# Moving the combine of expert rows ahead of the rotary products on VectorE, in the second half of an attention and mixture-of-experts kernel

## The reference

```python
xn = _layernorm(x, axis=-1)
x = x + attn(xn, W_qkv, W_o) + ffn(xn, router_w, router_b, w1, w2)
```

## Time and profile before

| | |
|---|---|
| median of 3 runs | 1364.79 us |
| profiled execution | 1371.59 us, its span 1369.8 us |
| TensorE matmul busy | 1246.6 us, 91% of the span |
| VectorE busy | 1135.5 us, 83% |
| ScalarE busy | 1118.9 us, 82% |
| GpSimd busy | 957.0 us, 70% |
| mean granted TensorE clock | 0.97 of full speed |

### The profile page before, as it was taken

The page is one execution under the profiler, slowest core; times in us unless marked ns, Lnnn a source line. Parts: engine busy times, 40 slices in busy tenths (PEclk is TensorE's granted clock), DMA queues, the critical chain, the costliest instruction groups (busy, mean ns, idle before and its releaser), DMA issues.

```text
span 1369.8 us, 46659 instructions
## 1 busy us (share of the span) xinstructions
PE 1246.6 (91%) x15156; PEld 945.7 (69%) x15157; DVE 1135.5 (83%) x3911; ACT 1118.9 (82%) x3608; POOL 957.0 (70%) x1349
## 2 busy tenths in 40 slices
PE   1537999999999999998999999899999999999998
PEld 1514677777777777667898998566766777777766
DVE  5889888888888888876777777899999998898885
ACT  6517889898898899886787887888888888888885
POOL 3116888998998889883222221788888888888885
PEclk9558999999999999998999999999999999999999
DMA  9992433333433433353444443333334333443331
GB/s 290 290 274 70 111 81 79 81 80 80 97 95 82 98 92 79 80 140 105 126 128 130 124 130 89 84 83 88 87 94 103 97 87 95 103 104 88 88 89 31
DMA packets 154041, 149.07 MB, mean 109 GB/s; under 512 B 12785, under 2 KB 113521, under 8 KB 153585
## 3 DMA queue, kind: packets, MB, share of 16 engines
q1 hardware_dynamic: 145264, 129.21, 37.4%
q0 software_dynamic: 8576, 17.33, 4.4%
HBM read 38.28 MB, written 41.09 MB: 58 GB/s over the span
## 4 chain that ended last, share of the span: by engine, by line
PE 49%; DVE 25%; issue 11%; ACT 7%; POOL 4%; DMA 3%; SPq 2%; DVEq 0%; ACTq 0%; POOLq 0%
PE bank L1171 9%; PE bank L1172 9%; PE bank L1173 8%; DVE arena L1025 7%; PE bank L1253 6%; PE bank L1242 6%; PE bank L1280 5%; ACT probs L712 4%; DVE arena L981 4%; PE bank L1264 2%; DVE inv_parts L1039 2%; DVE arena L986 2%; DVE arena L980 2%; PE bank L1281 2%; ACT arena L656 2%
## 5 line engine op out<-in xcount | busy, mean ns | idle before, releaser
L712 ACT ACTIVATE probs<-arena,neg_max 128x128 f32<-128x128 f32 (+1 forms) x1024 | 454.0, 448 | 75.9 <-DVE neg_max L1025 72.5
L1025 DVE CUSTOM_DVE_ANT_0 arena<-bank,causal 128x128 f32<-128x128 f32 (+1 forms) x1024 | 302.8, 351 | 40.5 <-PE bank L1242 37.7
L1253 PE MATMUL bank<-ident,probs 128*128 128x128 f32 x1536 | 211.4, 274 | 7.3 <-DVE probsT L1047 3.3
L1253 PEld LDWEIGHTS bank<-ident,probs 128*128 128x128 f32 x1536 | 175.8, 141 | 37.2 <-issue 12.9
L513 POOL TENSOR_TENSOR arena<-o_whole,arena 128x256 f16<-128x256 f32 x256 | 181.5, 709 | 21.1
L712 ACT ACTIVATION_READ_ACCUMULATOR probs<-arena,neg_max 128x1 f32 x1024 | 196.0, 191 | 0.0
L1172 PE MATMUL bank<-arena 128*128 (+1 forms) x864 | 184.8, 239 | 0.0
L1171 PE MATMUL bank<-arena 128*128 (+1 forms) x864 | 183.6, 239 | 0.9 <-DVE arena L1145 0.8
L1242 PE MATMUL bank<-arena 64*128 64x128 f16 (+1 forms) x3072 | 172.1, 245 | 9.7 <-DVE neg_max L1025 5.2
L1173 PE MATMUL bank<-arena 128*128 (+1 forms) x864 | 180.8, 238 | 0.0
L695 ACT ACTIVATE probsT<-bank 128x384 f32<-128x384 f32 x384 | 170.5, 480 | 0.9
(11 more groups left out here) (154 smaller groups left out, 3310.8 us busy)
## 6 DMA issues: line engine op xcount, KB each, us to landing
arena<-arena SPq DMA_DIRECT2D x256, 256.0 KB, 3.8
arena<-sorted_x_dram SPq DMA_DIRECT2D x144, 128.0 KB, 2.2
sorted_x_dram<-stage SPq DMA_DIRECT2D x6, 2304.0 KB, 17.8
sorted_y_dram<-stage SPq DMA_DIRECT2D x72, 128.0 KB, 1.8
sorted_x_dram<-stage SPq DMA_DIRECT2D x2, 2368.0 KB, 19.1
arena<-experts_dram SPq DMA_DIRECT2D x8, 512.0 KB, 6.6
out_dram<-acc SPq DMA_DIRECT2D x32, 128.0 KB
sorted_x_dram<-stage,slots POOLq DMA_INDIRECT x128
```

The lines of the kernel that those rows point to most:

```text
L712: last = nc.scalar.activation(probs[:, s % 4, at:at + w], masked[:, s % 4, at:at + w], ACT.Exp, bias=neg_max[:, s % 4, t:t + 1], scale=-1. ...
L1025: last = nc.vector.tensor_tensor_reduce(out=masked[:, (s + i) % 4, at:at + w], in0=SC[i][:, at:at + w], in1=causal[:, 2 * P - w:2 * P], sc ...
L1253: last = nc.tensor.transpose(TP[s % 2][:, k * P:(k + 1) * P], probs[:, s % 4, k * P:(k + 1) * P], ident[:])
```

## The change

On VectorE, in the second half, the combine of a period is issued directly behind `masks` and `invert` and ahead of `turn` and `o_scale`; before, it stood behind `turn`, `o_scale` and `rope_low`. The lag stays 2 (`BACK_LAG`), and the combines of `rest_of` stay where they are. In one line the constant's name takes the place of the number 2.

```diff
-                    then = past(b, p, 2)
+                    then = past(b, p, BACK_LAG)
                     if then and p % 2 == 0:
                         invert(4 * then[0] + then[1] // 2, then[1] // 2)
+                    if then and b >= MID:
+                        combine(*then)
                     for kind, j, of, u, psum in units_at(b, p):
                         if kind == "rope":
                             turn(j, u, psum, of)
...
                     for kind, j, of, u, psum in due(b, p, 2):
                         if kind == "rope" and j >= 2 and b <= MID:
                             rope_low(j, of)
-                    then = past(b, p, BACK_LAG)
-                    if then and b >= MID:
-                        combine(*then)
                     for kind, j, of, u, psum in units_at(b, p):
                         if kind == "y":
                             y_add(of, j, u, psum, at in (FORMER, TURN))
```

## The result

| | before | changed |
|---|---|---|
| median of 5 runs | 1364.79 us (1364.40 to 1366.27) | 1371.49 us (1370.76 to 1373.22) |
| profiled execution, its span | 1371.59, 1369.8 us | 1373.22, 1371.4 us |
| mean granted clock | 0.97 | 0.97 |

The ratio is 1.0048, 95% interval [1.0033, 1.0062]: slower by 6.7 us. Two later comparisons of the same two kernels gave 1.0017 [1.0005, 1.0029] and 1.0020 [1.0008, 1.0032], that is 2.3 and 2.7 us. The kernel before never again had a median as low as 1364.79: in later jobs it was 1368.34, 1367.88, 1368.27 and 1374.41. So 2 to 3 us is what repeats. I predicted +2.0 us.

The account below looks back on a forecast made before the run. TensorE bounds the second half, VectorE sets most of its losses. Per sample +0.4 us wait in p3, -0.2 transposes; 12 samples +2.4, first two -0.5: total +2, 1366.8 us, range 1353.5 to 1370.5.

Parts of the forecast that it names:

- the case in which the combine of p1 slips in: Second half, p1: combine starts 0.04 us ahead of GpSimd's L513, gets in, holds it some 0.15; likeliest case.
- The hold: VectorE's combine is held until GpSimd's instruction ends, finishing 0.14 or 0.15 us after it, rather than slowed.
- rival D: Contention is a slowdown: combine costs 0.70 us ahead of `turn` too; 1377 us; chance 0.08 together with a gather wait.
- What it saves: VectorE 0.44 us per `turn` period; L970 down to 0.34 to 0.45; TensorE's 0.2 before p3's transposes, L986 wait gone.
- What p6 and p0 pay: Combine ahead of `turn` makes `turn` 0.26 us late in p6 and 0.47 late in p0.
- rival A: In p1 the combine is held by L513; `turn` of p2 is 0.55 us late; 1368.5 us; chance 0.24.
- A's sum: Second half: 12 samples each 0.35 us longer, less 0.5 for its first two samples: +3.7, 1368.5 us.
- The bound on the masks: In p6, masks wait for TensorE; if they came 0.3 us sooner, the sum would be 3.6 lower.
- The gather: VectorE's wait for gathered rows moves up by 1.5 us at most; gather issued two periods before; costed at nothing.
- B: String breaks at p2: L1039 gets in before L513; 30.9 us a sample, 1353.5; chance 0.28 with halves of it.
- The base: Profiled execution of 1371.59 us is 6.8 above the median of 1364.79; the difference is carried over to the median.
- My own sign: Prediction is wrong if p3's output units are not 31.7 to 32.3 us apart, or TensorE stops elsewhere than p3.

Follow-up runs that it names:

- the sixteen columns: Kernel before, with a combine that adds only the first 16 of the 128 columns; one run, 1364.28 us, 31.12 us a sample.
- the run later by one: Kernel before, combines still behind `o_scale`, those of p2, p3 and p4 one period later, two in p5; 1361.53 us, ratio 0.9958.
- the second profile: Changed kernel run and profiled again with nothing edited, against the kernel before in the same job; 1370.07 us, ratio 1.0017.

## Why the prediction was right or wrong

It said 1366.8 us, +2.0 over 1364.79, by the case in which the combine of p1 slips in. Measured was 1371.49, outside the range. Point by point:

- **The hold** was right, and the sixteen columns show it by themselves. The Trainium skill has it the same way on another page than the one that rival D reads as a slowdown: it (SBUF — State Buffer, section SBUF: two separate sides) calls the shared pair an exclusive lock, held for the whole instruction, in which the loser is fully blocked. The ends 0.14 us after GpSimd's instruction agree with that.
- **What it saves**: L970 from 674 to 456 ns (I said 0.34 to 0.45 us), and the transposes' 0.2 gone (0.25 in the run later by one). Right, but part of L970's time went to L1041. The wait for L986 is another matter: where the masks are early it is 1.5 us in the kernel before and 1.6 changed, so there was nothing to save; only where they are late does it fall, from 3.9 to 1.6.
- **What p6 and p0 pay**: I had 0.26 and 0.47. Measured are 0.27 and 0.40 where the masks are early, 0.28 and 0.50 where they are late, if one takes off the 0.20 by which the masks themselves are later. Right.
- **p1 is the step that failed.** I took it that a combine starting 0.04 us ahead of L513 slips in and holds it by 0.15. The arrival was right (I had 0.03 ahead of L513, the rows show 0.02 to 0.04), the outcome not: the combine was held by L513, and L513 wasn't moved at all (0.48 after L511, 0.47 in the earlier trace rows). That is rival A, which had 0.24 of my chances, in its place, its price (`turn` of p2 0.55 late, measured 0.50) and its sign. My point from which A decides, 0.04 us later than my times, was drawn too late: a lead of 0.04 isn't enough, one of 0.06 is, and the 0.15 is then right. In the sum the step is small: `turn` of p2 is 0.50 late and not 0.4, some 1.2 us in 12 samples.
- **A's sum** was 12 x 0.35 - 0.5 = +3.7. Measured is 0.24 a sample in one kind of chip and 0.50 in the other. The 0.24 is 0.49 - 0.25, against my 0.55 - 0.2. The 0.50 has a term that I didn't have: the masks of p6 come 0.20 later than before. My reading, which no run tests, is that TensorE had lost that much in the waits for L986 and ahead of the transposes, and that with these gone its results come later behind its rows instead.
- **The bound on the masks** ("if they came 0.3 sooner, the sum would be 3.6 lower") has a right size, 0.26 x 12 = 3.1, but the wrong cause. The change doesn't move them forward; on other chips they come 0.4 us sooner in the kernel before, and 0.6 in the changed one.
- **The gather** I costed at nothing on the strength of one wait of 0.6 us. In the second profile VectorE waits for it six times, 3.2 us in 380; 1.0 to 1.4 us is passed on where the masks are early. A mis-sized term: the combine now asks up to 1.5 us sooner, and the gather of two periods before has not always landed.
- **B** was wrong in its place (L1039 of p2 starts 0.27 behind L513, not 0.10) but its pace was there to be had: 30.67 a sample, once the combines leave p0, p1 and p2 altogether and L1039 gets in ahead of L518.
- **D** falls with the sixteen columns.
- **The base.** Where the masks are late, the profile gave 31.8 us a sample and 1371.6; the median of 1364.79 belongs to other executions, which have no profile. I carried the difference over as if it were constant. Of the first 6.7 us some 3 repeat. The rest stays unexplained: later jobs had the kernel before at 1368 and 1374 us, and a copy of it 0.15% from itself in one job.
- **My own sign** was 31.7 to 32.3 us a sample. It is 31.64 where the masks are early, outside, and 32.29 where they are late as in the profile that I predicted from, just inside.

So the step that failed is p1, where the combine was held and L513 was not, and beside it two terms were mis-sized: the gather at nothing (1.0 to 1.4 us), and the masks of p6, which I took to stay where they were (0.20 us a sample on the late kind). The second half came out 3.2 us longer on one kind of chip and 4.4 on the other, against my 2.0. That +2.0 lies so near the 2.3 and 2.7 us of the later comparisons is in part luck. What took the first comparison to 6.7 us nothing later repeated, and its cause stays open.

## What to carry to other kernels

If an instruction with two SBUF inputs is held by GpSimd, moving it ahead of the work that starts GpSimd saves its own time but puts it on the string; move it to a period where nothing waits behind it instead. One period later gained 0.4% here with the buffers as they were, and eight buffers in place of four allowed a move that gained 0.56%. A start a few hundredths of a microsecond ahead of the rival's in a trace is not a won race (78 of 78 were lost here at 0.02 to 0.04 us): price such a tie as lost. And read the wait on the far side of a moved instruction in more than one execution, best on more than one chip, before a single profile is trusted.

## Not expected

- VectorE's combine, arriving in a gather 0.31 us ahead of L496, was held over L496 and L497 as well: 1.89 us for 0.34 of work. In the changed kernel a lead of 0.04 over L513 lost too, and GpSimd's instruction was not late by it. The Trainium skill (the page and section named above) says that whichever starts first gets the pair for the whole instruction; by the start that a row shows, these two cases are against it, and the one with a lead of 0.06 agrees. Why a lead of 0.31 was lost, from within a gather, stays open.
- A gather isn't always clear. Most combines inside one take 0.34 or 0.35 us, but in the kernel before one that starts 0.40 into a gather ends 0.24 after the gather's end, inside L496.
- A second combine directly behind a held one is held again, by the next of GpSimd's instructions: two in 1.81 us.
- TensorE's rows can hide a lag. In two of five jobs, each on its own chip, its results reach VectorE 0.4 us later than on the others between p5 and p6, with the same starts in its own rows and no gap. Why, stays open. It makes the same kernel 31.79 instead of 31.40 us a sample.
- The kernel before, by job: 1364.79, 1368.34, 1367.88, 1368.27, 1374.41 us. A difference of 0.2% can be read only within a job, and barely there.
